# Attention's prologue in a macaron kernel: who prepares the first four tiles, and in which order

## The reference

```python
x = x + 0.5 * ffn(layernorm(x))
x = x + attn(layernorm(x))
x = x + 0.5 * ffn(layernorm(x))

def attn(x):                                  # 8 sequences of 512 rows, 16 heads of 8
    Q = x @ wq + bq; K = x @ wk + bk; V = x @ wv + bv
    Q, K, V = [t.reshape(B * H, S, D) for t in (Q, K, V)]
    scores = einsum('bqd,bkd->bqk', Q, K) / sqrt(D)
    ctx = einsum('bqk,bkd->bqd', softmax(scores), V).reshape(B, S, E)
    out = ctx @ wo + bo + x
    return layernorm(out) * gamma + beta
```

## Time and profile before

| what | us |
|---|---|
| median of 3 runs | 854.29 |
| lowest and highest of them | 851.5, 857.88 |
| the profiled execution's own time | 853.64 |
| its span in the trace | 851.9 |
| busy in the span: PE, DVE, ACT, POOL | 684.0, 614.0, 455.7, 396.4 |

### The profile page before, as it was taken

The page is one execution under the profiler, slowest core; times in us unless marked ns, Lnnn a source line. Parts: engine busy times, 40 slices in busy tenths (PEclk is TensorE's granted clock), DMA queues, the critical chain, the costliest instruction groups (busy, mean ns, idle before and its releaser), DMA issues.

```text
span 851.9 us, 16015 instructions
## 1 busy us (share of the span) xinstructions
PE 684.0 (80%) x5121; PEld 310.5 (36%) x5121; DVE 614.0 (72%) x1577; ACT 455.7 (53%) x1052; POOL 396.4 (47%) x528
## 2 busy tenths in 40 slices
PE   4885686604899999999999999999998548667770
PEld 3643454402133333333333333333323425344550
DVE  4798744344968889899898998989983859863330
ACT  5752222201167778777787777878778334222220
POOL 5575877756413224243342433424201347577862
PEclk9997656765579999999999999999999669675555
DMA  7997443335524454444534444454411210643334
GB/s 194 243 241 201 93 73 66 43 67 113 86 47 77 97 99 83 98 92 92 102 84 94 96 97 99 81 99 94 100 39 45 50 38 9 176 89 60 63 42 111
DMA packets 233734, 80.34 MB, mean 94 GB/s; under 512 B 166888, under 2 KB 226440, under 8 KB 233608
## 3 DMA queue, kind: packets, MB, share of 16 engines
q1 hardware_dynamic: 217160, 67.04, 35.8%
q0 software_dynamic: 12288, 10.49, 8.4%
q10 hardware_dynamic: 4224, 2.10, 0.9%
HBM read 49.94 MB, written 31.49 MB: 96 GB/s over the span
## 4 chain that ended last, share of the span: by engine, by line
PE 45%; POOL 16%; issue 14%; DVE 13%; ACT 5%; DMA 5%; POOLq 0%; DVEq 0%; ACTq 0%
PE psum L1577 13%; PE psum L1586 12%; PE psum L1564 10%; POOL sums L640 8%; POOL arena L615 4%; DMA sums<-sums_sb,sidx 3%; DVE arena L1011 3%; ACT arena L1331 2%; PE psum L1531 1%; PE psum L1526 1%; ACT z_sb L1316 1%; DVE arena L1024 1%; PE psum L1380 1%; PE psum L1396 1%; DVE arena L785 1%
## 5 line engine op out<-in xcount | busy, mean ns | idle before, releaser
L1011 DVE TENSOR_REDUCE arena<-psum 128x2 f32<-128x1024 f32 x256 | 308.6, 1216 | 45.4 <-PE psum L1564 42.4
L1331 ACT ACTIVATE arena<-psum 128x512 f32<-128x512 f32 x512 | 285.3, 602 | 104.0 <-PE psum L1577 101.5
L1564 PE MATMUL psum<-arena 72*128 72x512 bf16 x512 | 201.5, 400 | 4.0 <-DVE arena L1011 3.2
L1577 PE MATMUL psum<-arena 74*128 74x512 bf16 x512 | 197.8, 389 | 4.0 <-ACT arena L1331 2.1
L1586 PE MATMUL psum<-arena 128*32 128x512 f32 x1024 | 137.3, 608 | 1.1 <-ACT arena L1331 0.5
L640 POOL DMA_INDIRECT sums<-sums_sb,sidx x64 | 103.6, 1619 | 41.4 <-issue 18.3
L1577 PEld LDWEIGHTS psum<-arena 74*128 74x128 bf16 x512 | 50.8, 100 | 147.9 <-ACT arena L1331 119.5
L690 POOL CAST arena<-arena 128x256 bf16<-128x256 f32 x32 | 12.7, 396 | 192.5 <-issue 188.5
L615 POOL DMA_INDIRECT arena<-dispatch_rows,arena x64 | 64.1, 1002 | 29.9 <-issue 18.3
L1449 PE MATMUL psum<-ident,arena 128*128 128x128 f32 x64 | 25.8, 421 | 48.7 <-DMA arena<-dispatch_rows,arena 48.5
L1564 PEld LDWEIGHTS psum<-arena 72*128 72x128 bf16 x512 | 50.0, 100 | 38.5 <-DVE arena L1011 15.1
(11 more groups left out here) (142 smaller groups left out, 1139.9 us busy)
## 6 DMA issues: line engine op xcount, KB each, us to landing
arena<-qk_parts SPq DMA_DIRECT2D x128, 96.0 KB
ctx<-arena SPq DMA_DIRECT2D x32, 256.0 KB, 2.0
qk_parts<-arena SPq DMA_DIRECT2D x32, 192.0 KB, 3.8
arena<-lists SPq DMA_DIRECT2D x16, 256.0 KB
sums<-x_sb SPq DMA_DIRECT2D x16, 256.0 KB
arena<-qk_parts SPq DMA_DIRECT2D x64, 64.0 KB
arena<-ctx SPq DMA_DIRECT2D x64, 64.0 KB, 2.7
wgu_sb<-in_L_ffn_w_gate SPq DMA_DIRECT2D x8, 384.0 KB, 4.4
```

Of the source, the lines that this page charges most:

```text
L1011: dve.tensor_reduce(mx_r[r % 2][:, 2 * p:2 * p + 2], src, X, ALU.max).then_inc(a_mx, 1)
L1331: act.activation(p_r[tau % NPB], bank[4 + tau % 2][:, :], ACT.Exp, scale=SCALE).then_inc(a_P, 1)
L1564: ins = pe.matmul(bank[tau % 4][:, :], heads(q_st[r], rows, g)[:, qt * P:(qt + 1) * P], heads(k_st[r], rows, g), start=True, stop=True)
L1577: pe.matmul(bank[4 + tau % 2][:, :], keys, heads(q_st[r], rows, g), start=True, stop=True)\
```

## The change

Four things are done to the prologue of attention, and nothing else in the kernel.

1. DVE's `next_stats(0, True)` aggregates each tile of group 0 right after its statistics. POOL takes the root for tile 0 alone, centres tile 0, takes the root for tiles 1 to 3, centres tile 1, and only then writes the residual operands of both (`root`, `normal`, `residual`); tiles 2 and 3 follow at once.
2. The splits of tiles 0 to 3 are done by DVE, each ahead of `v_copy` of its tile; POOL keeps the splits from tile 4 on, and does `center(4)` ahead of them.
3. For tiles 0 to 2, three of the eight stack loads (the key loads of the first two stack blocks) are issued by ACT (`keys_load`), after `qk_copy` of the next tile and after a wait for the stored parts; SP issues the other five.
4. PE does `prep(3)` ahead of `scores` of tile 0.

The diff, without blank lines:

```diff
@@ -449,7 +449,7 @@
                     sp.dma_start(parts_dram[r].rearrange("g c p s -> p (g c) s"),
                                  part_r[r % 2].rearrange("p (c s) -> p c s", s=HS)).then_inc(a_pst, 16)
-                def stack_load(t, r):
+                def stack_load(t, r, shared=False):
                     wait_each(sp, (a_ST, 16 * (t - 3)), (a_pst, 16 * t + 16))
                     parts = parts_dram[r].rearrange("g c (d j) s -> (c d) g (j s)", d=HD)
@@ -458,6 +458,8 @@
                         first = b * NPART * HD
                         sp.dma_start(q_st[r][first:first + NPART * HD, :], parts[0:NPART * HD]).then_inc(a_stk[r], 16)
                         kept = (NPART - b) * HD
+                        if shared and b < 2:
+                            continue
                         sp.dma_start(k_st[r][first:first + kept, :], parts[(NPART + b) * HD:2 * NPART * HD])\
                           .then_inc(a_stk[r], 16)
                         if b:
@@ -482,7 +484,7 @@
                 sp.wait_ge(s_kini, 1)
                 for t in range(3):
                     stack_store(t, t)
-                    stack_load(t, t)
+                    stack_load(t, t, shared=True)
                 stack_store(3, 3)
                 max_rows(0, 0)
                 def step(n, r, end=NT):
@@ -646,11 +648,15 @@
                     return
                 clear_stacks()
                 pool.wait_ge(s_watt, 16 * 13)
-                for g in range(NG):
-                    if g in (2, 4, 6):
-                        center(g // 2 - 1, g // 2 - 1)
-                    if g in (3, 5):
-                        split(g // 2 - 1, g // 2 - 1)
+                root(0, 1)
+                normal(0, 0)
+                root(1, GT)
+                normal(1, 1)
+                residual(0, 0)
+                residual(1, 1)
+                for t in (2, 3):
+                    normal(t, t)
+                    residual(t, t)
             def clear_stacks():
@@ -660,20 +666,31 @@
             def center(t, r):
+                if t == GT:
+                    root(GT, NT)
+                normal(t, r)
+                residual(t, r)
+            def root(first, last):
+                nth = {1: 1, GT: 2, NT: 3}[last]
+                pool.wait_ge(a_aggr, last)
+                pool.tensor_scalar(rstd[:, first:last], mv[:, first:last, 1], LN_EPS, None, ALU.add).then_inc(a_ve, 1)
+                pool.wait_ge(a_ve, nth)
+                pool.tensor_tensor(rstd[:, first:last], rstd[:, first:last], power[:, first:last], ALU.pow).then_inc(a_rs, 1)
+                pool.wait_ge(a_rs, nth)
+            def normal(t, r):
                 xt = x_sb[:, bass.ds(t, 1), :].rearrange("p a d -> p (a d)")
-                if isinstance(t, int) and t in (0, GT):
-                    last = GT if t == 0 else NT
-                    pool.wait_ge(a_aggr, last)
-                    pool.tensor_scalar(rstd[:, t:last], mv[:, t:last, 1], LN_EPS, None, ALU.add).then_inc(a_ve, 1)
-                    pool.wait_ge(a_ve, 1 if t == 0 else 2)
-                    pool.tensor_tensor(rstd[:, t:last], rstd[:, t:last], power[:, t:last], ALU.pow).then_inc(a_rs, 1)
-                    pool.wait_ge(a_rs, 1 if t == 0 else 2)
                 wait(pool, a_use, use("x", t - 2) + 1 if not isinstance(t, int) or t >= 2 else 0)
+                wait(pool, a_zb, t - 1)
                 pool.tensor_tensor(xn_r[r % 2], xt, mv[:, bass.ds(t, 1), 0].to_broadcast([P, D]), ALU.subtract)\
                     .then_inc(a_xc, 1)
                 pool.wait_ge(a_xc, t + 1)
                 pool.tensor_tensor(xn_r[r % 2], xn_r[r % 2], rstd[:, bass.ds(t, 1)].to_broadcast([P, D]), ALU.mult)\
                     .then_inc(a_xn, 1)
+            def residual(t, r):
+                xt = x_sb[:, bass.ds(t, 1), :].rearrange("p a d -> p (a d)")
                 pool.wait_ge(a_xn, t + 1)
                 pool.tensor_tensor(z_sb[:, bass.ds(t * P, P)], xn_r[r % 2], bo_sb[:], ALU.add).then_inc(a_zb, 1)
                 pool.tensor_tensor(xt, xt, beta_sb[:], ALU.add).then_inc(a_xb, 1)
@@ -686,6 +703,8 @@
                 waits = [(a_read, use("q", t) + 1)]
                 if not isinstance(t, int) or t >= 2:
                     waits.append((a_pst, 16 * (t - 1)))
+                if t == GT:
+                    waits.append((a_parts, GT))
                 wait_apart(pool, *waits)
                 pool.tensor_copy(p1, qk).then_inc(a_part1, 1)
                 pool.wait_ge(a_part1, t + 1)
@@ -707,9 +726,8 @@
                     z = z_sb[:, g * GT * P:(g + 1) * GT * P].rearrange("p (i d) -> p i d", i=GT)
                     pool.wait_ge(a_zn, GT * (g + 1))
                     pool.tensor_tensor(z, z, gamma_sb[:].unsqueeze(1).to_broadcast([P, GT, P]), ALU.mult).then_inc(a_fin1, 1)
-                split(2, 2)
-                center(3, 3)
-                for t in range(3, NT):
+                center(GT, 0)
+                for t in range(GT, NT):
                     n = t - 4
                     split(t, t % NBUF)
                     if t + 1 < NT:
@@ -758,6 +776,21 @@
                 b = bv_sb[:].rearrange("p (k c) -> p k c", k=4).unsqueeze(1).to_broadcast([P, NH, 4, HD])
                 dve.tensor_tensor(v_r[r][:, :, :, 0:HD], bank[7][:, 0:P].rearrange("p (g k c) -> p g k c", g=NH, k=4),
                                   b, ALU.add).then_inc(a_read, 1)
+            def split(t, r):
+                p1, p2, p3 = [part_r[r % 2].rearrange("p (g qk c s) -> p c qk g s", g=NH, qk=2, c=NPART)[:, c]
+                              for c in range(NPART)]
+                qk, res = [b[r % 2].rearrange("p (qk g s) -> p qk g s", qk=2, g=NH) for b in (qk_r, res_r)]
+                dve.wait_ge(a_read, use("q", t) + 1)
+                wait(dve, a_pst, 16 * (t - 1))
+                dve.tensor_copy(p1, qk).then_inc(a_part1, 1)
+                dve.wait_ge(a_part1, t + 1)
+                dve.tensor_tensor(res, qk, p1, ALU.subtract).then_inc(a_res1, 1)
+                dve.wait_ge(a_res1, t + 1)
+                dve.tensor_copy(p2, res).then_inc(a_part2, 1)
+                dve.wait_ge(a_part2, t + 1)
+                dve.tensor_tensor(p3, res, p2, ALU.subtract).then_inc(a_parts, 1)
             def neg_mean(f, g):
                 tiles = slice(g * GT, (g + 1) * GT)
@@ -975,12 +1008,14 @@
                         indices(1)
                 assert step[0] == totals["list_step"], step[0]
-                def next_stats(g):
+                def next_stats(g, now=False):
                     dve.wait_ge(s_xl[g], 16)
                     for j in range(GT):
                         dve.bn_stats(stats[:, bass.ds(g * GT + j, 1), :].rearrange("p a c -> p (a c)"),
                                      x_sb[:, bass.ds(g * GT + j, 1), :].rearrange("p a d -> p (a d)")).then_inc(a_stat, 1)
+                        if now:
+                            variance(j, j + 1, a_stat, a_aggr)
                 if f.p == 1:
                     return
@@ -991,15 +1026,17 @@
                 for i in range(2):
                     dve.tensor_copy(wqk_sb[:, i * D:(i + 1) * D].rearrange("k (d j) -> k d j", d=HD),
                                     wqk_raw[:, i * D:(i + 1) * D].rearrange("k (j d) -> k d j", d=HD)).then_inc(s_wqk, 1)
-                for g in range(NG):
+                next_stats(0, True)
+                for g in (1, 2):
                     next_stats(g)
-                    if g == 0:
-                        variance(0, GT, a_stat, a_aggr)
-                    if g == 4:
-                        dve.wait_ge(s_vini, 1)
-                    if g in (4, 5, 6):
-                        v_copy(g - 4, g - 4)
+                dve.wait_ge(s_vini, 1)
+                for t in range(3):
+                    split(t, t)
+                    v_copy(t, t)
+                    next_stats(3 + t)
+                split(3, 3)
+                next_stats(6)
+                next_stats(7)
             def attention():
                 variance(GT, NT, a_stat, a_aggr)
@@ -1317,9 +1354,20 @@
                                          scale=rstd[:, t:t + 1], bias=negm[:, t:t + 1])
                     if t % GT == GT - 1:
                         ins.then_inc(f.xn.sem, 1)
+                def keys_load(t, r):
+                    act.wait_ge(a_pst, 16 * t + 16)
+                    parts = parts_dram[r].rearrange("g c (d j) s -> (c d) g (j s)", d=HD)
+                    act.dma_start(k_st[r][0:3 * HD, :], parts[3 * HD:6 * HD]).then_inc(a_stk[r], 16)
+                    act.dma_start(k_st[r][3 * HD:5 * HD, :], parts[4 * HD:6 * HD]).then_inc(a_stk[r], 16)
+                    act.dma_start(k_st[r][5 * HD:6 * HD, :], parts[3 * HD:4 * HD]).then_inc(a_stk[r], 16)
+                act.wait_ge(s_kini, 1)
                 for t in range(NBUF):
                     xT_copy(t, t)
                     qk_copy(t, t)
+                    if 1 <= t:
+                        keys_load(t - 1, t - 1)
                 max_copy(0, 0)
```

(3 more changed lines are left out.)

## The result

| | before | changed |
|---|---|---|
| median of 21 runs each, us | 854.59 | 859.75 |
| lowest, highest | 851.5, 860.36 | 858.08, 863.37 |
| ratio, with its 95% interval | | 1.0054 [1.0036, 1.0072] |
| span of the profiled execution | 851.9 | 856.4 |

The changed kernel is slower by 3.1 to 6.2 us, 4.6 in the middle; forecast were 3.5, and 857.1 for its time, in a range of 851.8 to 861.8.

The account below looks back on a forecast made before the run. PE sets the steady steps; the prologue hangs on DVE's first row maximum. It comes 4.8 us late, less 1.0 and 0.3 for two waits: 3.5 us on 853.64 gives 857.1, range 851.8 to 861.8.

Parts of the forecast that it names:

- The start: Before the first transpose: fewer statistics and aggregates and a one-column root for tile 0 gain 1.2 us.
- The split on DVE: Splits of tiles 0 to 3: two subtractions and two casts on DVE take 1.8 us, against 2.43 on POOL.
- D: Length of one tile's split on DVE, taken as 1.8 us, with bounds 0.9 and 3.0.
- The port: Split 0 on DVE beside POOL's operations: port sharing adds 0.6 us, within 0 to 1.6.
- The period: Time from one tile's transpose to the next falls from 6.16 to 4.9 us, but for four tiles.
- The key loads on ACT: ACT's loads and their wait for tile 1's store delay the copy of tile 3's transpose: cost 1.1 us.
- Tile 3 first: Split, statistics and aggregates before the maxima make DVE 4.8 us late; two vanished waits (DVE 1.01, PE 0.28) give back 1.3.
- Step 0: First attention step on PE: starts 3.5 us later, near 235, and is as long as before, 17.6 us.
- Cheap hand-overs (1): Prologue: split 1.3 us and ACT never blocks, so maxima 1.1 us late, time 853.4, no change; chance 0.2.
- Faster by the clock (2): Step 0: PE's clock reaches its upper level by its start, saving 4.4 us, time 852.7; chance 0.12.
- A later rise (3): Attention's first steps: PE's clock rises a step later, costing 4.4 us, time 861.5; chance 0.1.
- The dear end (4): Prologue: split 3.0 us and port wait 1.6, so maxima 9.5 us late, time 861.8; chance 0.08.

Follow-up runs that it names:

- e7_port: Changed kernel with POOL's residual operands and the centrings of tiles 2 and 3 held back until DVE's splits 0 and 1 are done; ratio to before 1.0052.
- e1_keys_sp: Changed kernel with all eight stack loads of tiles 0 to 2 issued by SP again; ratio to before 1.0005.
- e4_stats_early: Changed kernel with the statistics of groups 3 to 7 and all 28 aggregates put into DVE's waits before split 3; ratio to before 1.0043.
- e8_clock: e5_combined with extra float32 matmuls on PE after v of tiles 0 to 2 and between scores of tiles 0 and 1; ratio to before 0.9937.
- e6_comb_act: e5_combined with the three key loads of tiles 0 to 2 issued by ACT; ratio to before 0.9964.
- e12_before_keys: Kernel before with only three of the eight stack loads of tiles 0 to 2 issued by ACT; ratio to before 0.9987.
- e10_pv_ahead: e5_combined with the edit of e7_port, plus extra four-matmul groups after the last four score pairs of tile 1; ratio to before 0.9916.
- e5_combined: Changed kernel with key loads on SP, tile 3 after tile 0's scores and its split on POOL, statistics and aggregates in DVE's waits; ratio to before 0.9944.
- the other two edits: Changed kernel's key loads put back on SP; tile 3 prepared after tile 0's scores with its split on POOL. With early statistics, ratio to before 0.9944.

## Why the prediction was right

**Right in sign, in size to 0.8 us of the stretch, and in where the loss is made.** DVE's first maximum comes late because tile 3 and ACT's key loads stand ahead of it. One term, the wait of ACT, was mis-sized by a factor of three; part of that was made up by chance, by terms that were priced too high. Each step against what was measured, all counted from the first statistic:

- *The start.* Forecast gain 1.2; the first transpose is at 2.73 against 3.83: 1.10.
- *The split on DVE.* D was taken as 1.8; it is 1.54 (0.29 + 0.43 + 0.29 + 0.43 and the waits). The casts were over-priced by the lack of a row of their width.
- *The port.* 0.6 was added to split 0; e7_port shows 0.59. The 0.6 was picked between 0 and 1.6, so that the figure fits this well is luck; that POOL's operations are the cause is shown.
- *The period.* The second and third transposes were forecast at 8.2 and 13.1 and came at 8.07 and 12.69.
- *The key loads on ACT.* This is the term that was mis-sized: 1.1 us forecast, 3.23 measured by e1_keys_sp. The prediction had the store of tile 1 go out at 13.9 and land 4.39 us later, as in the earlier trace rows, at 18.3. It landed at 19.80. That it went out at 14.85 (SP's first three load issues took 2.50 us, one of ACT's 1.39) is not the cause: in e4_stats_early and e7_port it went out at 13.42 and 12.85 and landed at 20.19 and 19.57. The step that failed is to take the landing as a fixed time after the issue; it went with the moment at which the loads ahead of it began, in every trace. In the kernel before it is 20.83 - 12.91 = 7.92 us after the first load, and the same figure would have given 11.55 + 7.92 = 19.5. The rest of the 3.23 is that without the loads the copy would have begun at 17.80 (e1_keys_sp) and not at 18.5. The copy of tile 2, which I had called free, was 0.9 us late, and that did not matter at the end: it is on time in e4_stats_early and e7_port, and the copy of tile 3 begins 0.39 us later and 0.23 sooner there.
- *Tile 3 first.* Statistics and aggregates were priced at 3.6 us and took 3.4. The first maximum was forecast at 27.3 and came at 28.14. Two waits were to give back 1.3; they gave 5.66 - 4.31 = 1.35.
- *Step 0* as before: 17.40 against 17.50, and no steady step changed.

The sum of the step 0 shift was 3.5 and is 4.31. ACT's copy of tile 3 began at 21.02 and not 19.56, 1.46 later: the landing is 1.5 us later, and the cheaper splits of tiles 0 to 2 (0.8 us in all) do not help, for what DVE saves ahead of a store is waited for on ACT. Behind that copy, split 3, the statistics and the aggregates gave 0.6 back.

**The rivals.** Cheap hand-overs (1): the split came near its price of 1.3, but its other condition, that ACT never blocks, failed; in e1_keys_sp, where it holds, the stretch is 1.08 us longer than before, where that rival had it 0.2 shorter; the time, 1.0005 of before, cannot tell the two apart. Faster by the clock (2): no trace of the changed order showed an early rise, and e8_clock shows that more work of that kind did not bring it. A later rise (3) happens: in e6_comb_act and e12_before_keys, two of the fourteen traces, the clock rose only 22 to 23 us after the transpose of tile 4, where it was 10 to 12 in the others but e10_pv_ahead, and step 0 lasted 21.7 us, some 4.3 more than before. One is the kernel before with the key loads on ACT, the other a combined one, and the changed kernel's own trace has it at 11.8 us; whether the change makes a late rise more frequent, these runs are too few to say. The dear end (4) was not reached.

**What stays open.** Why one DMA issue in the prologue takes some 1.1 us more than its like (ACT 1.39, SP 1.60, 1.48, 1.62 in different places; none among the stores and loads of the parts in five of the seven traces with key loads on ACT), and what decides whether the clock rises 10 or 20 us into the steps. Nor was it tested what sets the landing of the store of tile 1 beside the loads of tile 0, and whether splits 0 to 2 on POOL would serve e5_combined as they serve the changed kernel. The 1.4 us that the profiled pair differs by after attention was not tested.

## What to carry to other kernels

When a stage is set by a serial prologue, find the engine whose first bulk operation starts the steady pace (here DVE's row maxima) and count everything that stands ahead of it in its own order; in the changed kernel the splits on DVE, which is faster at them, cost 2.3 us of the stretch more than on the slower helper beside it, and one more tile ahead of it cost 1.5 us on the kernel before. A wait for a transfer should never stand in the order of an engine ahead of a short operation that others wait for: alone the key loads on ACT were free, and with tile 3 behind them they cost 3.2 us. Use the waits of the bounding engine for work that is due later: the same statistics and aggregates, placed there, brought the first maximum 2.5 us forward, and together with the other two edits took the kernel from 0.5% over to 0.6% under. And do not count a store's landing from its issue when loads are in flight: here it came 0.2 us sooner when the store went out 2.0 us sooner.

## What the runs showed of the hardware

The granted clock did not follow how busy PE was. With PE busy for 21.34 of 22.81 us, on bf16 matmuls of 72 rows and short float32 ones, it stayed at 0.50 (e8_clock); in e10_pv_ahead it went to 1.00 some 3.5 us after the first of four extra groups of float32 matmuls, four side by side from 128 rows onto 32 columns each. That is one run. Step 0 holds such groups of its own: in eleven of the thirteen traces without the extra ones the clock rose 1.4 to 3.6 us after the first of them began, in e6_comb_act and e12_before_keys 14 us after; so the form alone does not fix the moment. ACT's first issue of a key load took 0.63 or 0.64 us in each of the seven traces that have it, and 0.32 for the same load of the next tile. SP issued at the same moment both times, so SP's issue is not what makes it long. A 192 KB store was hardly sooner in DRAM for going out sooner behind loads: it landed 7.7 to 9.0 us after the first of them in fourteen traces, issued 1.9 to 4.3 us after it.
